# Turning quantized tokens: two DMA transposes per tile in place of eight TensorE transposes

## The chip, the cores and the metric

The kernel runs on one core of a Trainium2 chip. The metric is the device time of one execution in microseconds (us), the median of three runs. A change of under 0.5% (3.2 us here) can't be told from no change.

## The reference

The input `x` is 64 batches of 64 channels by 1024 positions. Two layers follow each other. Cut to what matters for this change, the first one is:

```python
def _L0_cond_ref(x, c, weight, c_weight, bias):      # grouped convolution, 4 groups, 9 taps, pad 4
    out = lax.conv_general_dilated(x, weight, (1,), [(4, 4)], dimension_numbers=('NCH', 'OIH', 'NCH'), feature_group_count=4)
    return out + jnp.einsum('nd,od->no', c, c_weight)[:, :, None] + bias[None, :, None]

def _L0_ffn_ref(input_act, weight):                  # 8 bit quantized dense layer over the 1024 positions
    w_scale = max(abs(weight), axis=-1) / 127;  w_q = round(weight / w_scale)
    a_scale = max(abs(input_act), axis=-1) / 127;  x_q = round(input_act / a_scale)
    return (x_q @ w_q.T * a_scale * w_scale.T).astype(float16)

x = x + _L0_ffn_ref(_L0_cond_ref(x, ...), L0_ffn_weight)
x = x + _L1_ffn_ref(_L1_cond_ref(x, ...), ...)       # per batch 64x64 channel mixing, then a dense layer with a low-rank term
```

A token is one batch and channel (4096 in all), a row of 1024 positions. The dense layer contracts over positions. Its left operand on TensorE must therefore have positions on the partitions and tokens along the free dimension. The convolution leaves the opposite: partitions hold 8 position phases by 16 channels, and the free dimension holds, for each of 8 sets (2 batches by 4 groups), 128 positions of one phase. So each tile has to be turned between the convolution and the integer product, and this step is what changes.

## The kernel before

The work is cut into 32 tiles of two batches (128 tokens). All five engines run hand-written instruction lists. The main loop has one pass for each `c` from 3 to 31. In pass `c`, TensorE (PE) does in this order: the convolution of tile c (`conv`, L462), the channel mixing of tile c-3 (`mix`, L505), the integer product of tile c-2 (`int_product`, L521, 16 matmuls of 512 columns) with the small `row_total` (L485) after the first four and `max_rows` (L528) after eleven, then `max_back` (L532), then `tokens_out` of tile c-1 (L493, the eight transposes) and, in odd passes from 5 on, `rank_pair` (L552, L555). After the loop comes a second stage in which TensorE does the last tiles and then the dense products of layer two (L584, L770); it lasts from 312 us to the end.

Beside it, within a pass:

- VectorE (DVE) adds the bias to the convolution's result (L1245), takes row maxima (L1251), computes the scale of tile c-3 (L1281 to L1288), scales the first half of the product (`layer0(c-2, 0)`, L1277), and then does `chan_max(c)` (L1256, L1257), `low` (L1293), `scales(c)` (L1262, L1263, L1268), and `layer0(c-2, 1)` (L1277 again). DVE works strictly in this order.
- ScalarE (ACT) does `row_sums` (L841), one or two weight steps, `high` twice (L856), `tokens_sb(c-1)` (L846), and `scale_rows(c)` (L863, eight instructions that write `yv`).
- GpSimd (POOL) adds layer one's result to `x` (L1088).
- SyncE (SP) issues DMAs: per pass `save_x1` (L307), which waits for POOL, `save_x2` (L311), the next `x_phases` (L259) and `x` (L263), and in part of the passes a weight tile (L319, L326). One queue keeps them in the order of issue.

The path of a tile's tokens: `scale_rows(t)` in pass t rounds the numbers by adding a large constant, and leaves them in `yv` as f32 words whose lower half is a float16. In pass t+1, TensorE transposes eight 128x128 blocks of these halves into a PSUM bank, and ACT copies the bank into `yq_both` in bf16, taking away the constant. In pass t+2 `int_product` loads `yq_both` as stationary operand. `max_back` brings the channel maxima back to the partitions: DVE makes an 8x128 tile from 8 rows, TensorE turns it into a 128x8 one.

Two waits matter below. `max_back` waits for `chan_max` (semaphore `chanmax_ready`). And `conv(t)` waits, ahead of its third group (g = 2), for `f_ready` 2t-4, that is for `layer0(t-3, 1)`: the second half of the product lies in the PSUM bank that these groups write. In passes with a `rank_pair` that product lies between `max_back` and the next convolution, in the others nothing but `tokens_out` does.

## Time and profile before

| | |
|---|---|
| median of 3 runs | 648.31 us (647.93 to 650.51) |
| profiled execution, span | 646.6 us |
| rest (median less span) | 1.7 us |
| PE busy | 623.8 us, 96% |
| DVE, ACT, POOL busy | 418.3, 335.3, 336.2 us |
| main loop, passes 3 to 31 | some 45 to 312 us |
| DMA | 138.38 MB, mean 214 GB/s |

The profiled execution's own time is given only as its span, from the first to the last instruction; what lies around it is taken as the difference to the median. "PE" is the matmul row and "PEld" the loads of stationary operands, which run ahead of the matmuls. A busy PE is not one at its peak, so gaps in the PEld rows, and the distance from one group's first load to the next one's, say more of what an instruction costs than busy time does. A start is in us from the span's start. "[0.42 <-X]" is an idle time ahead of an instruction, and what ended it.

### The profile page before, as it was taken

The page shows a single profiled execution, that of the slowest core. Times are in us where ns is not written, and L with a number is a line of the kernel's source. Part 1 is how long each engine was busy: PE and PEld are TensorE (multiplying, and loading weights), DVE is VectorE, ACT ScalarE, POOL GpSimd, SP SyncE. Part 2 cuts the span into 40 slices and gives each one's busy share as a digit, 9 for nine tenths or more (in the row PEclk, how much of TensorE's full clock was granted, in tenths as well). Part 3 has the DMA queues.
Part 4 walks back from the last instruction along what each step waited for, and adds up shares of the span by engine and source line. Part 5 has one row for each costly group of instructions (what it writes and reads, how often), then busy time and mean ns, then how long its engine had stood idle before and what let it go on. Part 6 is the DMA issues. An engine that isn't in the chain of part 4 may idle for free.

```text
span 646.6 us, 14948 instructions
## 1 busy us (share of the span) xinstructions
PE 623.8 (96%) x5865; PEld 337.3 (52%) x5898; DVE 418.3 (65%) x891; ACT 335.3 (52%) x566; POOL 336.2 (52%) x223
## 2 busy tenths in 40 slices
PE   7789999999999999999999999999999999999997
PEld 5556565566566666656554444444444444444443
DVE  5958778877787778787537797745544433444434
ACT  2857898667778777776652436334333313333100
POOL 3012222217778522225485689886866678666400
PEclk8799999999999999999999999999999999999999
DMA  8969877677799797764529014554555433457103
GB/s 299 361 137 365 295 284 273 233 266 276 280 342 336 285 359 280 259 229 140 217 73 357 35 34 153 206 203 156 196 195 193 158 132 136 162 197 259 66 1 130
DMA packets 46707, 138.38 MB, mean 214 GB/s; under 512 B 13180, under 2 KB 13468, under 8 KB 46465
## 3 DMA queue, kind: packets, MB, share of 16 engines
q1 hardware_dynamic: 41886, 120.65, 52.6%
q10 hardware_dynamic: 4752, 16.78, 6.4%
q8 instruction: 47, 0.77, 0.5%
q14 instruction: 22, 0.18, 0.1%
HBM read 89.13 MB, written 48.28 MB: 213 GB/s over the span
## 4 chain that ended last, share of the span: by engine, by line
PE 51%; DVE 1%; issue 0%; ACT 0%; DVEq 0%
PE ps L770 36%; PE ps L584 9%; PE ps L752 2%; PE ps L521 2%; PE ps L505 1%; PE ps L462 0%; PE ps L552 0%; DVE z_lo L1304 0%; DVE unscale L1441 0%; DVE ring L1293 0%; DVE yb L1245 0%; DVE zT L1306 0%; PE ps L555 0%; PE ps L730 0%; PE ps L493 0%
## 5 line engine op out<-in xcount | busy, mean ns | idle before, releaser
L1088 POOL TENSOR_TENSOR x<-x_in,f_both 128x512 f32<-128x512 f32 x64 | 74.0, 1157 | 195.9 <-DVE f_both L1277 195.9
L521 PE MATMUL ps<-wqT,yq_both 128*128 128x512 bf16 x479 | 113.2, 379 | 6.0 <-issue 4.6
L462 PE MATMUL ps<-x_ph,conv_w 64*64 64x256 f32 (+1 forms) x1024 | 98.2, 396 | 2.2 <-DMA conv_w<-in_conv_taps 2.0
L863 ACT ACTIVATE yv<-yb,yinv 128x128 f32<-128x128 f32 x256 | 78.0, 389 | 2.3 <-DVE yinv L1268 2.2
L902 ACT ACTIVATE ring<-ring,ratio 128x2048 f16<-128x2048 f16 x26 | 50.6, 1994 | 51.1 <-DVE wst L1537 14.1
L770 PE MATMUL ps<-ffn_wT,ring 128*128 128x512 f16 x312 | 71.6, 379 | 0.0
L462 PEld LDWEIGHTS ps<-x_ph,conv_w 64*64 64x64 f32 (+1 forms) x1024 | 51.1, 137 | 37.4 <-issue 14.2
L521 PEld LDWEIGHTS ps<-wqT,yq_both 128*128 128x128 bf16 x512 | 45.2, 97 | 48.4 <-issue 1.0
L1245 DVE TENSOR_TENSOR yb<-ps,ybias 128x1024 f32<-128x1024 f32 x32 | 39.1, 1223 | 41.1 <-PE ps L462 41.0
L584 PE MATMUL ps<-ffn_wT,ring 128*128 128x512 f16 x288 | 64.6, 379 | 0.0
L856 ACT ACTIVATE ring<-ps,t_up 128x512 f16<-128x512 f32 x64 | 40.5, 683 | 45.5 <-issue 38.1
L1119 POOL TENSOR_TENSOR bias_b<-ring 128x1024 f32<-128x1024 f16 x13 | 27.8, 2137 | 48.4 <-ACT ring L902 48.2
L1550 DVE SCALAR_TENSOR_TENSOR x_in<-ps,unscale,x_in 128x512 f32<-128x512 f32 x30 | 22.5, 750 | 43.7 <-PE ps L770 43.5
L1277 DVE SCALAR_TENSOR_TENSOR f_both<-ps,tok_scale,wsc_b 128x512 f16<-128x512 f32 x64 | 47.8, 748 | 4.1 <-PE ps L521 3.3
L770 PEld LDWEIGHTS ps<-ffn_wT,ring 128*128 128x128 f16 x312 | 30.5, 98 | 36.8
L846 ACT ACTIVATE yq_both<-ps 128x1024 bf16<-128x1024 f16 x32 | 32.7, 1023 | 31.3 <-PE ps L493 31.0
L1293 DVE SCALAR_TENSOR_TENSOR ring<-ps,t_up,ring 128x512 f16<-128x512 f32 x64 | 46.9, 737 | 0.8 <-ACT ring L856 0.8
L584 PEld LDWEIGHTS ps<-ffn_wT,ring 128*128 128x128 f16 x288 | 27.2, 98 | 32.1 <-issue 0.8
L1550 DVE SCALAR_TENSOR_TENSOR wst<-ps,unscale,wst 128x512 f32<-128x512 f32 x28 | 21.0, 750 | 35.2 <-PE ps L770 35.1
L1251 DVE TENSOR_REDUCE rowmax<-yb 128x8 f32<-128x1024 f32 x32 | 39.0, 1220 | 1.0
L505 PEld LDWEIGHTS ps<-mixT,x 64*64 64x64 f32 x2048 | 35.8, 135 | 5.2 <-issue 1.6
L1550 DVE SCALAR_TENSOR_TENSOR x<-ps,unscale,x 128x512 f32<-128x512 f32 x21 | 15.8, 750 | 31.1 <-PE ps L770 31.1
(284 smaller groups left out, 1096.6 us busy)
## 6 DMA issues: line engine op xcount, KB each, us to landing
x_ph<-in_x_phases SPq DMA_DIRECT2D x32, 516.0 KB, 6.1
x_in<-in_x SPq DMA_DIRECT2D x32, 512.0 KB, 6.4
x_scratch<-x SPq DMA_DIRECT2D x32, 512.0 KB, 2.8
x_scratch<-ring SPq DMA_DIRECT2D x26, 512.0 KB, 4.1
ring<-x_scratch SPq DMA_DIRECT2D x26, 512.0 KB, 4.3
wst<-in_w_rows SPq DMA_DIRECT2D x12, 512.0 KB, 5.0
x_in<-x_scratch SPq DMA_DIRECT2D x12, 512.0 KB, 6.5
out<-x_in ACTq DMA_DIRECT2D x12, 512.0 KB, 3.6
```

What stands on the lines that cost most here:

```text
L462: return mm(ps_conv[o, g * 2 * MB:(g + 1) * 2 * MB], conv_w[k, g, w.start + o.start:w.start + o.stop], xp[k, g, :, view], start=first, sto ...
L505: last = mm(bank(2 + e)[j * 64:(j + 1) * 64, k * CH:(k + 1) * CH], x1[b, t % 2, l:l + 64], mixT[b, t, b], start=True, stop=True)
L521: last = mm(acc_bank(t, h), yqT[:, t % 2, p, :], wqT[:, p, h * HALF:(h + 1) * HALF], start=p == 0, stop=p == PH - 1)
L584: last = mm(o, x2_cols[:, x2_slot(n), a, k, :], ffn_wT[:, w, k, h * HALF:(h + 1) * HALF], start=k == 0 and i == 0, stop=k == NL - 1 and i ...
L770: last = mm(b, left(a, k), right(w, k), start=fresh and k == 0 and i == 0, stop=k == 3 and i == 2, skip_group_check=True)
L856: A(x2_cols[:, t % RING, 0, :, h * CH:(h + 1) * CH], bank(2 + h).rearrange("p (c t) -> p c t", c=NL), ACT.Copy, scale=t_up[:, t % 4:t % 4 ...
L863: last = A(yv[:, s, :], yb[:, t % 2, s, :], ACT.Copy, scale=yinv[:, s:s + 1], bias=MAGIC)
L902: A(cols, cols, ACT.Copy, scale=ratio[:, t:t + 1]).then_inc(sem("norm_ready"), 1)
L1088: g.tensor_tensor(x1[:, t % 2, s], x_in[:, t % 3, s], f16[:, s], ALU.add).then_inc(sem("x1_ready"), 1)
L1277: v.scalar_tensor_tensor(f16[:, s], acc_bank(t, h), tok_scale[:, t % 4:t % 4 + 1], wsc_b[:, s], ALU.mult, ALU.mult).then_inc(sem("f_ready" ...
L1293: v.scalar_tensor_tensor(x2_cols[:, t % RING, 1, :, cols], bank(2 + h).rearrange("p (k t) -> p k t", k=NL), t_up[:, t % 4:t % 4 + 1], x2_c ...
L1550: v.scalar_tensor_tensor(buf, src, unscale[:, t:t + 1], buf, ALU.mult, ALU.add).then_inc(sem("pair_folded"), 1)
```

## The change

For tiles 2 to 31 the transposes leave TensorE. ACT writes `yv` less the constant as bf16 into a new tile `yq_out` (`tokens_whole`), at the place where it copied the PSUM bank before. SP then issues two DMA transposes of 64x1024 each into `yq_both` (`turn_tokens`), and `int_product` waits for both. Tiles 0 and 1 (`EARLY = 2`) are turned on TensorE as before.

A DMA transpose of 64 rows gives tokens in another order than the eight TensorE transposes did, so the rows of the convolution's output are reordered: the partition is now (half, channel, phase in the half) where it was (phase, channel). The taps, the bias weights and `fside` are laid out for it ahead of the kernel, and the product's left operand is read with a step of four elements. The scale of a token was found with a masked sum over `ps_small` and `set_mask`; in the new order it comes from a second small product (`chanmax_tok` by `ones8`) in `max_back`, for which `chan_max` has one more instruction.

```diff
+            def turn_tokens(t):
+                sp.wait_ge(sem("yq_ready"), t + 1 - EARLY)
+                wait(sp, "acc_ready", 2 * (t - 1))
+                for h in range(2):
+                    sp.dma_start_transpose(yq_both[:, t % 2, h * HALF:(h + 1) * HALF].rearrange("m (s r) -> m s r", s=8),
+                                           yq_out[h * CH:(h + 1) * CH, :]).then_inc(sem(f"yqT_moved{t % 2}"), 16)
+
             for c in range(1, NT + 3):
+                if c == NT:
+                    turn_tokens(NT - 1)
...
+                if EARLY < c < NT:
+                    turn_tokens(c - 1)
                 if c == NT:
                     fetch_x1(0)
                     load_t(1)
...
             def int_product(t, h, lo=0, hi=PH):
                 if lo == 0:
-                    wait(pe, "yqT_ready", t + 1)
+                    if t < EARLY:
+                        pe.wait_ge(sem("yqT_ready"), t + 1)
+                    else:
+                        pe.wait_ge(sem(f"yqT_moved{t % 2}"), 32 * ((t - EARLY) // 2 + 1))
...
-                    last = mm(acc_bank(t, h), yqT[:, t % 2, p, :], wqT[:, p, h * HALF:(h + 1) * HALF], start=p == 0, stop=p == PH - 1)
+                    last = mm(acc_bank(t, h), yqT[:, t % 2, p // 4, :, p % 4], wqT[:, p, h * HALF:(h + 1) * HALF], start=p == 0, stop=p == PH - 1)
...
             def max_back(t):
-                wait(pe, "chanmax_ready", t + 1)
-                tr(ps_small[:, 128:136], chanmax_rep[:, :, :].rearrange("p a c -> p (a c)"), ident[0:8, 0:8]).then_inc(sem("max_psum"), 1)
+                wait(pe, "chanmax_ready", 2 * t + 2)
+                tr(ps_small[:, 128:136], chanmax_rep[:, :, :, :].rearrange("p h c q -> p (h c q)"), ident[0:8, 0:8])
+                mm(ps_small[:, 136:137], chanmax_tok[:, :, :].rearrange("p s c -> p (s c)"), ones8[:, :], start=True, stop=True).then_inc(sem("max_psum"), 1)
...
                 max_back(c)
-                tokens_out(c - 1)
...
+            def tokens_whole(t):
+                wait(act, "yv_ready", t + 1)
+                if t > EARLY:
+                    act.wait_ge(sem(f"yqT_moved{(t - 1) % 2}"), 32 * ((t - 1 - EARLY) // 2 + 1))
+                A(yq_out[:, :], yv[:, :, :].rearrange("p s m -> p (s m)"), ACT.Copy, bias=-WHOLE).then_inc(sem("yq_ready"), 1)
...
-                tokens_sb(c - 1)
+                tokens_whole(c - 1)
                 scale_rows(c)
 
+            tokens_whole(NT - 1)
             t_high(0)
...
             def chan_max(t):
...
+                v.tensor_tensor(chanmax_tok[:, :, :], chanmax[:, :].unsqueeze(1).to_broadcast([8, 8, CG]),
+                                ident[0:8, 0:8].unsqueeze(2).to_broadcast([8, 8, CG]), ALU.mult).then_inc(sem("chanmax_ready"), 1)
...
-                v.tensor_tensor_reduce(tok_junk[:, :], ps_small[:, 128:136], set_mask[:, :], scale=1.0 / QMAX, scalar=0.0,
-                                       op0=ALU.mult, op1=ALU.add, accum_out=tok_scale[:, t % 4:t % 4 + 1]).then_inc(sem("tok_scale_ready"), 1)
+                v.tensor_scalar(tok_scale[:, t % 4:t % 4 + 1], ps_small[:, 136:137], 1.0 / QMAX, None, ALU.mult).then_inc(sem("tok_scale_ready"), 1)
```

TensorE before, from one pass with a `rank_pair` to the next convolution (L532 is `max_back`, L493 the eight transposes, L552 and L555 the rank pair, L462 the convolution, L505 the mixing, L521 the integer product):

```order
L521 MATMUL ps<-wqT,yq_both 128x512 x5
L532 MATMUL ps<-ident,chanmax_rep 128x8
L493 MATMUL ps<-identh,yv 128x128 x8
L552 MATMUL ps<-ring,z_w 104x256 x8
L555 MATMUL ps<-ring,z_w 40x256 x8
L462 MATMUL ps<-x_ph,conv_w 64x256 x16
L505 MATMUL ps<-mixT,x 64x64 x32
```

The same place after (lines of the changed program: L549 and L550 are `max_back`, L568 and L571 the rank pair, L476 the convolution, L519 the mixing):

```order
L538 MATMUL ps<-wqT,yq_both 128x512 x5
L549 MATMUL ps<-ident,chanmax_rep 128x8
L550 MATMUL ps<-ones,chanmax_tok 128x1
L568 MATMUL ps<-ring,z_w 104x256 x8
L571 MATMUL ps<-ring,z_w 40x256 x8
L476 MATMUL ps<-x_ph,conv_w 64x256 x16
L519 MATMUL ps<-mixT,x 64x64 x32
```

The eight transposes are gone and one small product stands behind `max_back`'s transpose.

VectorE before, around `chan_max` and `scales`:

```order
L1277 SCALAR_TENSOR_TENSOR f_both<-ps,tok_scale,wsc_b 128x512
L1256 TENSOR_REDUCE chanmax<-ps 8x16
L1257 TENSOR_TENSOR chanmax_rep<-ps,chanmax 8x128
L1293 SCALAR_TENSOR_TENSOR ring<-ps,t_up,ring 128x8x64
L1262 TENSOR_SCALAR yscale<-ps 128x8
L1263 ISA tok_junk,tok_scale<-ps,set_mask 128x8
L1263 ISA tok_scale 128x1
L1268 RECIPROCAL yinv<-yscale 128x8
L1277 SCALAR_TENSOR_TENSOR f_both<-ps,tok_scale,wsc_b 128x512
```

And after (L1300 is `layer0`, L1316 `low`):

```order
L1300 SCALAR_TENSOR_TENSOR f_both<-ps,tok_scale,wsc_b 128x512
L1278 TENSOR_REDUCE chanmax<-ps 8x16
L1279 TENSOR_TENSOR chanmax_rep<-ps,chanmax 8x128
L1281 TENSOR_TENSOR chanmax_tok<-chanmax,ident 8x128
L1316 SCALAR_TENSOR_TENSOR ring<-ps,t_up,ring 128x8x64
L1286 TENSOR_SCALAR yscale<-ps 128x8
L1287 TENSOR_SCALAR tok_scale<-ps 128x1
L1291 RECIPROCAL yinv<-yscale 128x8
L1300 SCALAR_TENSOR_TENSOR f_both<-ps,tok_scale,wsc_b 128x512
```

One instruction more stands ahead of `low`, and the masked sum with its readout has become one `TENSOR_SCALAR`.

SyncE before, one pass (the saves of x1 and x2, two loads, a weight tile):

```order
L307 DMA x_scratch<-x 128x1024
L311 DMA x_scratch<-ring 128x1024
L259 DMA x_ph<-in_x_phases 128x1032
L263 DMA x_in<-in_x 128x1024
L319 DMA wst<-in_w_rows 128x1024
```

And after:

```order
L310 DMA x_scratch<-x 128x1024
L314 DMA x_scratch<-ring 128x1024
L262 DMA x_ph<-in_x_phases 128x1032
L266 DMA x_in<-in_x 128x1024
L322 DMA wst<-in_w_rows 128x1024
L373 DMA_TRANSPOSE yq_both<-yq_out 128x8x64 x2
```

The two transposes stand behind the pass's loads and ahead of the next pass's saves.

## Rows read from the trace of the kernel before

**Rows 1.** The page, part 1: engine, busy us, share of the span, instructions.
```profile
PE 623.8 (96%) x5865; PEld 337.3 (52%) x5898; DVE 418.3 (65%) x891; ACT 335.3 (52%) x566; POOL 336.2 (52%) x223
```

**Rows 2.** Waits from 50 to 320 us: who <- for whom: total us, times, longest.
```profile
ACT yq_both L846 <- PE ps L493: 25.8, 24, 1.4
PEld ps L532 <- DVE chanmax_rep L1257: 12.5, 29, 0.6
...
PEld ps L462 <- DVE f_both L1277: 3.9, 14, 0.6
```

**Rows 3.** Timeline, a pass with a rank pair: start us, us, engine, line, operation.
```profile
199.38 1.24 ACT L856 ACTIVATE ring<-ps,t_up 128x512 f16<-128x512 f32 x2
...
200.76 0.13 PEld L532 LDWEIGHTS ps<-ident,chanmax_rep 8*128 8x128 f32 x1 [0.42 <-DVE chanmax_rep L1257]
...
200.91 0.45 PEld L493 LDWEIGHTS ps<-identh,yv 128*128 128x128 f16 x8
...
201.32 0.84 PEld L552 LDWEIGHTS ps<-ring,z_w 128*104 128x104 f16 x8
...
203.51 0.33 SPq L307 DMA_DIRECT2D x_scratch<-x  x1
...
206.57 0.55 PEld L521 LDWEIGHTS ps<-wqT,yq_both 128*128 128x128 bf16 x4
```

**Rows 4.** Timeline, the next pass, without a rank pair.
```profile
208.91 1.27 ACT L856 ACTIVATE ring<-ps,t_up 128x512 f16<-128x512 f32 x2 [0.86 <-issue]
...
209.70 0.28 DVE L1257 TENSOR_TENSOR chanmax_rep<-ps,chanmax 8x128 f32<-8x128 f32 x1
209.91 0.73 DVE L1293 SCALAR_TENSOR_TENSOR ring<-ps,t_up,ring 128x512 f16<-128x512 f32 x1
210.27 0.13 PEld L532 LDWEIGHTS ps<-ident,chanmax_rep 8*128 8x128 f32 x1 [0.42 <-DVE chanmax_rep L1257]
...
210.42 0.45 PEld L493 LDWEIGHTS ps<-identh,yv 128*128 128x128 f16 x8
...
210.57 0.14 DVE L1262 TENSOR_SCALAR yscale<-ps 128x8 f32<-128x8 f32 x1
...
210.98 0.63 PEld L462 LDWEIGHTS ps<-x_ph,conv_w 128*64 128x64 f32 x8
...
211.01 0.75 DVE L1277 SCALAR_TENSOR_TENSOR f_both<-ps,tok_scale,wsc_b 128x512 f16<-128x512 f32 x1
211.09 1.02 ACT L846 ACTIVATE yq_both<-ps 128x1024 bf16<-128x1024 f16 x1 [0.91 <-PE ps L493]
...
211.81 0.66 PEld L462 LDWEIGHTS ps<-x_ph,conv_w 128*64 128x64 f32 x8 [0.21 <-DVE f_both L1277]
...
215.15 0.55 PEld L521 LDWEIGHTS ps<-wqT,yq_both 128*128 128x128 bf16 x4
```

**Rows 5.** DMA issues by tile: count, KB each, median us to landing.
```profile
mixT<-agg_scratch SPq DMA_DIRECT2D x4, 256.0 KB, 4.3
...
out<-wst ACTq DMA_DIRECT2D x2, 256.0 KB, 2.2
```

**Rows 6.** The line of the mixT loads (L297), all four: duration ns, time to landing.
```profile
L297 SPq DMA_DIRECT2D mixT<-agg_scratch x4: 674/1332/1462, 33.9 to 37.4; - x4
...
DMA to landing us min/median/max: 3.5/4.3/4.7
```

**Rows 7.** Timeline of passes 4 and 8: the token copy and the next integer product.
```profile
63.99 1.02 ACT L846 ACTIVATE yq_both<-ps 128x1024 bf16<-128x1024 f16 x1
...
67.17 0.55 PEld L521 LDWEIGHTS ps<-wqT,yq_both 128*128 128x128 bf16 x4
...
101.14 1.02 ACT L846 ACTIVATE yq_both<-ps 128x1024 bf16<-128x1024 f16 x1
...
103.55 0.55 PEld L521 LDWEIGHTS ps<-wqT,yq_both 128*128 128x128 bf16 x4
...
105.59 0.18 PE L485 MATMUL ps<-x1sum,ones_b 128*128 128x1 bf16 x1 [0.99 <-ACT f_both L841]
```

**Rows 8.** Timeline, the last tile's transposes, after the loop.
```profile
320.02 0.65 PEld L493 LDWEIGHTS ps<-identh,yv 128*128 128x128 f16 x8
```

**Rows 9.** The line of the weight transposes (L431), loads with a step of 32 bytes.
```profile
L431 PEld LDWEIGHTS ps<-identh,ffn_wT x64: 140/151/168, 14.7 to 35.9; 128*128 128x128 f16 x64
```

More of the change, by code:

```diff
@@ L34 @@
 HALF_BIAS = 1536.0
-MAGIC = 12582912.0 + 0x6600
+WHOLE = 12582912.0
+MAGIC = WHOLE + 0x6600
 EXPMASK = 0x7F800000
 TOP = 13
+EARLY = 2
 RING = 6
@@ L91, in program @@
         yq = yv[:, :, :].bitcast(F16).rearrange("p s (m w) -> p s m w", w=2)[:, :, :, 0]
-        yqT = yq_both[:, :, :].rearrange("p a (s m) -> p a s m", s=PH)
+        yqT = yq_both[:, :, :].rearrange("m a (h n q) -> m a h n q", h=2, q=PH // 2)
+        yq_out = sb("yq_out", [P, L], BF16)
         f_both = sb("f_both", [P, 2, L], F16)
@@ L692, in _ @@
             int_product(NT - 2, 0)
-            tokens_out(NT - 1)
             int_product(NT - 2, 1)
@@ L845, in tokens_sb @@
                 wait(act, "acc_ready", 2 * (t - 1))
-                A(yqT[:, t % 2, :, :].rearrange("m p (s c) -> m s p c", s=8),
-                  ps_trh.rearrange("m (s p c) -> m s p c", s=8, p=PH), ACT.Copy, bias=-HALF_BIAS).then_inc(sem("yqT_ready"), 1)
+                A(yq_both[:, t % 2, :].rearrange("m (h s r) -> m s h r", h=2, s=8),
+                  ps_trh.rearrange("m (s h r) -> m s h r", s=8, h=2), ACT.Copy, bias=-HALF_BIAS).then_inc(sem("yqT_ready"), 1)
+            def tokens_whole(t):
[3 more added lines that the diff above has]
+                A(yq_out[:, :], yv[:, :, :].rearrange("p s m -> p (s m)"), ACT.Copy, bias=-WHOLE).then_inc(sem("yq_ready"), 1)
             def high(t, h):
@@ L860, in scale_rows @@
                 wait(act, "yinv_ready", t + 1)
-                wait(act, "yqT_psum", t)
+                wait(act, "yqT_psum", min(t, EARLY))
+                wait(act, "yq_ready", t - EARLY)
                 for s in range(8):
-                    last = A(yv[:, s, :], yb[:, t % 2, s, :], ACT.Copy, scale=yinv[:, s:s + 1], bias=MAGIC)
+                    last = A(yv[:, s, :], yb[:, t % 2, s, :], ACT.Copy, scale=yinv[:, s:s + 1], bias=MAGIC if t < EARLY else WHOLE)
                 last.then_inc(sem("yv_ready"), 1)
@@ L990, in _ @@
             t_scale(1)
-            tokens_sb(NT - 1)
             t_scale(2)
@@ L1059, in _ @@
             g = nc.gpsimd
+            g.memset(ones8[:, :], 1.0)
             g.memset(ident[:, :], 0.0).then_inc(sem("ident_zero"), 1)
@@ L1255, in chan_max @@
                 wait(dve, "max_psum", t)
-                link(v.tensor_reduce(chanmax[:, :], ps_small[0:8, 0:P].rearrange("p (a c) -> p c a", a=PH), AX.X, ALU.max))
-                v.tensor_tensor(chanmax_rep[:, :, :], ps_small[0:8, 0:P].rearrange("p (a c) -> p a c", a=PH),
-                                chanmax[:, :].unsqueeze(1).to_broadcast([8, PH, CG]), ALU.max).then_inc(sem("chanmax_ready"), 1)
+                rows = ps_small[0:8, 0:P].rearrange("p (h c q) -> p h c q", h=2, q=PH // 2)
+                link(v.tensor_reduce(chanmax[:, :], rows.rearrange("p h c q -> p c h q"), AX.XY, ALU.max))
+                v.tensor_tensor(chanmax_rep[:, :, :, :], rows, chanmax[:, :].unsqueeze(1).unsqueeze(3).to_broadcast([8, 2, CG, PH // 2]),
+                                ALU.max).then_inc(sem("chanmax_ready"), 1)
+                v.tensor_tensor(chanmax_tok[:, :, :], chanmax[:, :].unsqueeze(1).to_broadcast([8, 8, CG]),
+                                ident[0:8, 0:8].unsqueeze(2).to_broadcast([8, 8, CG]), ALU.mult).then_inc(sem("chanmax_ready"), 1)
             def scales(t):
@@ L1621 @@
         taps[v, :, 2:4, v:v + TAPS] = wc[:, 2:4]
+    taps = taps.reshape(PH, CG, GRP, 4, PH // 2, CG).transpose(0, 1, 2, 3, 5, 4)
     limes4 = _np.zeros((4, 4, E, 4, R), _np.float32)
@@ L1626 @@
         condT=f["cond_128"].T,
-        w_ctx=_np.broadcast_to(f["L0_cond_c_weight"].T.reshape(P, GRP, 1, CG), (P, GRP, PH, CG)).reshape(P, GRP * P),
-        fside=_np.tile(f["fside_S_0"].reshape(GRP, CG).T, (PH, 1)),
+        w_ctx=_np.broadcast_to(f["L0_cond_c_weight"].T.reshape(P, GRP, 1, CG, 1), (P, GRP, 2, CG, PH // 2)).reshape(P, GRP * P),
+        fside=_np.broadcast_to(f["fside_S_0"].reshape(GRP, CG).T.reshape(1, CG, 1, GRP), (2, CG, PH // 2, GRP)).reshape(P, GRP),
         mw0=f["L1_cond_W0"], mw1=f["L1_cond_W1"], mw2=f["L1_cond_W2"],
```

9 lines of the change are left out of this document (3 added, 6 removed).

## The prediction

> **What bounds the kernel now.** I read the page first: the reader is to see PE at 96% of the span while no other engine passes 65% [rows 1]. So TensorE's own list sets the time, and the question for each edit is what it does to the distance from one group of loads to the next on that engine. Next the waits inside the loop [rows 2]. Two of them hold TensorE: `max_back` waits for `chan_max` in all 29 passes, 12.5 us together, and the convolution waits 14 times (3.9 us) for the second half of `layer0`, which happens in the passes without a rank pair. ACT waits 25.8 us for the transposes, but nothing in these rows says that TensorE waits for what ACT does after them. Last, the timeline of one pass of each kind [rows 3, 4], to see what stands ahead of and behind the transposes.
>
> **What leaves TensorE.** In a pass with a rank pair the eight loads start at 200.91 and the next group at 201.32: 0.41 us [rows 3]. Without one it is 210.42 to 210.98, 0.56 us [rows 4]. The last tile's, in the stage behind the loop, take about 0.65 [rows 8], taken as 0.6. Taken by itself this is 14 x 0.41 + 15 x 0.56 + 0.6 = 14.7 us, and it is the whole of what the change can give.
>
> **What `max_back` gets.** The new small product has a load of the shape of L532's (8x128, f32, 0.13 us), and from that load to the next group passes 0.15 us (200.76 to 200.91) [rows 3]. It costs 0.15 us in each pass. The new DVE instruction has the shape of L1257, and from that one to the next instruction on DVE passes 0.21 us (209.70 to 209.91) [rows 4]. `max_back` waits for it too, and this wait is exposed already (0.42 us idle, rows 3 and 4), so 0.21 us is added to TensorE's idle time in full. The masked sum and its readout become one instruction; the reciprocal still waits for it, and I count nothing.
>
> In a pass with a rank pair the sum is -0.41 + 0.15 + 0.21 = -0.05 us. 14 of them: -0.7 us. Pass 3 has 16 small products behind `max_back` and counts the same.
>
> In a pass without one, TensorE comes to the next convolution 0.20 us earlier, but there it meets the wait that was binding before. `layer0` starts at 211.01, 0.44 us after `yscale` at 210.57, and ends at 211.76; the third group's load starts at 211.81 [rows 4]. `yscale` needs the result of `max_back`: 0.30 us after its load (210.27) before; now that load comes 0.21 later and the second product's 0.15 after it, so 0.36 us later. DVE is itself no longer busy then (`low` ends 0.21 later than 210.64). Taking 0.03 off for what DVE was late by before, `layer0` ends 0.33 us later and so does the load of the third group. TensorE's earlier arrival is spent waiting: the pass gets 0.33 us longer. 14 passes: +4.6 us.
>
> Ahead of the loop tile 2 meets the longer wait once, +0.4. The last tile's transposes leave -0.6. Together: -0.7 - 0.05 + 4.6 + 0.4 - 0.6 = +3.7 us. The gain of 14.7 us is gone before any DMA is counted, since 29 x 0.36 = 10.4 us goes to the small product and its input and the rest to the convolution's wait.
>
> **ACT.** `tokens_whole` takes the place of `tokens_sb` at about the same 1.02 us [rows 4] and no longer waits for TensorE: it starts when `high` ends, 0.9 us earlier (210.2 against 211.09). ACT's time isn't on the path, so this gives nothing in itself, but it starts the new DMA earlier.
>
> **The DMA transposes.** `int_product` now waits for them. Cover: in the pass without a rank pair, `high` ends at 210.18, the bf16 tile is there at 211.25, the product's first load stands at 215.15, 0.33 later after the change: 4.2 us. With one: 200.62, 201.7, 206.57: 4.9 us, about 5.1 where ACT is less loaded. SP is free at that moment, since it waits for POOL until 203.51 [rows 3]; behind the transposes on SP stand the saves, and they are late only if the issue takes over 1.8 us. The cover is less in early passes, where ACT has other work between `high` and the tokens: in pass 4, 67.17 less 65.05 is 2.1 us (2.4 with the later load), in pass 8, 103.55 less 102.2 is 1.3 us (1.7) [rows 7]; passes 5 to 7 lie between these and 4.2.
>
> No row shows a DMA transpose. From below: 256 KB in long rows landed 2.2 us after issue on a quiet queue [rows 5]. From above: a mixT load has the same 256 KB, in runs of 32 floats (128 bytes), which is also what a partition gets of one block here (64 tokens of 2 bytes); it took up to 1.46 us to issue and landed in 3.5 to 4.7 us, with four in flight [rows 6]; the sum of both is 6.2. The nearest row is the mixT load with the fewest ahead of it, so I take 3.5 us for the pair. Below the cover of 4.2 nothing is paid in 24 passes. Early passes pay: pass 4 1.1, pass 6 0.5, pass 8 1.8 less the 0.99 that TensorE waited there a moment later anyway (105.59) [rows 7], together 2.4 us.
>
> The VectorE page of the Trainium skill (VectorE: DVE Perf Modes, The three transpose paths) gives 1309 ns for a 128x128 bf16 block through DMA against 390 on TensorE, and its table says to use TensorE when PSUM will do. No run here shows the DMA figure. The eight blocks of this trace cost TensorE 0.41 to 0.56 us together, not 8 x 390 ns, so the price that the rule sets against the DMA is far too high here. By the page's figure, with the blocks one after another, a tile would take an estimated 10.5 us. The same skill (Advanced Engine Details and Errata, X-Bar Transpose) says that on this chip transposing DMAs are as fast as regular ones, which would make it the 2.2 us row.
>
> **Other edits.** The product reads its stationary operand with a step of 8 bytes. Loads with a step of 32 bytes took 0.15 us where others take 0.10 [rows 9, 4], and they lie beside matmuls of 512 columns; I count nothing. If that cover failed it would be up to 0.05 x 480 = 24 us. Layout changes of the taps cost nothing.
>
> **The sum.** On the profiled execution: 646.6 + 3.7 + 2.4 = 652.7 us of span, and with the 1.7 us between span and median 654.4 us.
>
> **Rivals.**
>
> 1. *The saving counts.* If the second small product and its input disappear in time that is idle anyway (the 0.42 us of `max_back`'s wait, if DVE's order gives it back), and only the 0.15 us load is paid, then 14.7 - 29 x 0.15 = 10.3 us is won less what early tiles pay: 640 us. For it speaks that TensorE is at 96% and that the instructions really leave its list. Against it: the 12.5 us wait on DVE and the 3.9 us wait of the convolution, both behind the point where the work is taken away. It decides if the third group's load comes no later than 1.5 us after `max_back`'s.
>
> 2. *The transposes land late.* At 5.6 us (1.33 issue plus 4.3) passes without a rank pair pay 1.4, those with one 0.5, the early ones 14 us together: 14.5 + 4.8 + 14 + 3.7 = +37, 685 us. At 5.0 us it is +23, 671 us. It gets worse in passes where weight loads were issued just before. From 4.2 us on it decides. If the eight blocks went one by one, at 10.5 us, each pass would be some 6 us longer, about +170 us; this is the case that the VectorE page's figure makes. For it: the short runs of [rows 6] are the nearest thing in the trace. Against it: each of the two DMAs has only half of a mixT load's bytes, and the four mixT loads were issued behind each other.
>
> 3. *Nothing to see.* The added wait is smaller than 0.21, or ACT's earlier finish helps TensorE in the early passes; the parts cancel within 3 us.
>
> **Chances.** Forecast (transposes mostly hidden, the gain eaten by the two waits, 650.5 to 660) 0.45. Rival 1 (637 to 645) 0.16. Rival 2 (above 660) 0.23, with 0.03 of it for the long end. Rival 3 (645 to 651.5) 0.16. 0.5% of 648.3 is 3.2 us, about what this measurement can tell from no change. So faster (below 645.1) 0.16; within it 0.22, rival 3 and the lower edge of the forecast; slower 0.62. For 8 in 10 the range goes from 643 (a part of rival 1 below it) to 674 (the upper part of rival 2 above it).
>
> **What would show it.** Right: `max_back`'s load waits about 0.63 us in place of 0.42; in passes without a rank pair the convolution's third group waits some 0.7 us for `layer0`; the pair of passes takes 0.28 us more; from ACT's bf16 tile to landing about 3.5 us; the first load of the product waits for DMA only in passes 4 to 8. Wrong: a wait of each product for `yq_both`, which is rival 2; passes shorter by 0.3 us or more, which is rival 1; loads of the product's left operand over 0.2 us.

## The result, and the profile after: 6.6% slower

| | before | after |
|---|---|---|
| median of 4 executions | 648.12 us (647.85 to 650.51) | 690.99 us (690.03 to 693.41) |
| profiled execution, span | 646.6 | 688.2 |

The ratio is 1.066, 95% interval 1.063 to 1.069. The direction was forecast. The size, +42.9 us where +6.1 was the sum, lies outside the range of 643 to 674.

The page's part 1 of after, against [rows 1]:

```profile
PE 629.0 (91%) x5689; PEld 341.6 (50%) x5722; DVE 443.4 (64%) x890; ACT 336.9 (49%) x566; POOL 336.4 (49%) x224
```

TensorE has fewer instructions than before and is as busy as before, but over a longer span. So it waits, and the waits from 50 to 320 us say for whom (total us, times, longest). On the load row of after, against [rows 2]:

```profile
PEld ps L549 <- DVE chanmax_tok L1281: 23.7, 25, 1.5
...
PEld ps L538 <- DMA yq_both<-yq_out: 11.9, 8, 2.5
...
PEld ps L476 <- DVE f_both L1300: 10.7, 14, 1.1
```

The same view for the matmul row of after, and then what it has on `max_back` for before:

```profile
PE ps L538 <- DMA yq_both<-yq_out: 12.5, 7, 2.7
PE ps L549 <- DVE chanmax_tok L1281: 11.8, 25, 1.0
PE ps L476 <- DVE f_both L1300: 4.4, 13, 0.7
PE ps L538 <- issue: 4.1, 12, 1.4
```

```profile
PE ps L532 <- DVE chanmax_rep L1257: 0.2, 1, 0.2
```

This last row is what the prediction had not read. The loads of `max_back` stood idle for 12.5 us before [rows 2], but the array behind them did not: its matmul row waited 0.2 us in all. After, both rows wait.

The pass without a rank pair of after, against [rows 4] (L1278, L1279 and L1281 are `chan_max`, L549 and L550 `max_back`, L867 `tokens_whole`):

```profile
212.86 0.28 DVE L1278 TENSOR_REDUCE chanmax<-ps 8x16 f32<-8x128 f32 x1
212.93 1.16 POOL L1110 TENSOR_TENSOR x<-x_in,f_both 128x512 f32<-128x512 f32 x1 [1.13 <-DVE f_both L1300]
213.11 1.06 ACT L867 ACTIVATE yq_out<-yv 128x1024 bf16<-128x1024 f32 x1
213.17 0.28 DVE L1279 TENSOR_TENSOR chanmax_rep<-ps,chanmax 8x128 f32<-8x128 f32 x1
213.38 0.85 DVE L1281 TENSOR_TENSOR chanmax_tok<-chanmax,ident 8x128 f32<-8x128 f32 x1
...
214.19 2.51 SPq L373 DMA_TRANSPOSE yq_both<-yq_out  x2
214.28 0.13 PEld L549 LDWEIGHTS ps<-ident,chanmax_rep 8*128 8x128 f32 x1 [0.86 <-DVE chanmax_tok L1281]
214.28 0.22 PE L549 MATMUL ps<-ident,chanmax_rep 8*128 8x8 f32 x1 [0.39 <-DVE chanmax_tok L1281]
214.29 0.35 PEld L550 LDWEIGHTS ps<-ones,chanmax_tok 8*128 8x128 f32 x2
...
214.66 0.63 PEld L476 LDWEIGHTS ps<-x_ph,conv_w 128*64 128x64 f32 x8
...
215.25 0.75 DVE L1300 SCALAR_TENSOR_TENSOR f_both<-ps,tok_scale,wsc_b 128x512 f16<-128x512 f32 x1
...
216.05 0.63 PEld L476 LDWEIGHTS ps<-x_ph,conv_w 128*64 128x64 f32 x8 [0.76 <-DVE f_both L1300]
...
220.58 0.58 PEld L538 LDWEIGHTS ps<-wqT,yq_both 128*128 128x128 bf16 x4 [1.25 <-DMA yq_both<-yq_out]
```

Three things are to be seen. `chanmax_tok` takes 0.85 us, not the 0.28 us of its neighbour of the same shape, and it ends (214.23) just after GpSimd's add (214.09). The two transposes keep SyncE's queue for 2.51 us. And the next product waits 1.25 us for their data: 220.58 is 6.4 us after the bf16 tile was there (214.17).

The line of the transposes, and that of `chanmax_tok`, over the whole execution (ns min/median/max):

```profile
L373 SPq DMA_TRANSPOSE yq_both<-yq_out x60: 1194/1257/2315, 58.9 to 352.3; - x60
...
DMA to landing us min/median/max: 2.6/3.8/7.1
```

```profile
L1281 DVE TENSOR_TENSOR chanmax_tok<-chanmax,ident x32: 268/854/958, 19.1 to 344.9; 8x128 f32<-8x128 f32 x32
```

And SyncE's queue (the page's part 3: packets, MB, share of 16 engines), before and then after:

```profile
q1 hardware_dynamic: 41886, 120.65, 52.6%
```

```profile
q1 hardware_dynamic: 74526, 128.52, 61.7%
```

52.6% of 646.6 us is 340.1, 61.7% of 688.2 us is 424.6. The 60 transposes added 84.5 us of all 16 DMA engines, 2.8 us a tile for 262 KB, and 544 packets each. At the rate of everything else on this queue (340.1 us for 120.65 MB) the same bytes would be 0.74 us.

Cutting the span at the first load of the product of pass 3 and of pass 31 shows where in the program the time lies. The experiments below are in the same table, each from its own trace:

| us | up to pass 3 | pass 3 to 31 | from there to the end | span |
|---|---|---|---|---|
| before | 50.3 | 256.0 | 340.3 | 646.6 |
| after | 54.3 | 287.3 | 346.6 | 688.2 |
| pe_turn | 53.6 | 277.5 | 341.1 | 672.2 |
| no_dma | 54.0 | 274.2 | 340.3 | 668.5 |
| unwaited | 52.9 | 272.6 | 346.5 | 672.0 |
| early | 51.8 | 273.2 | 340.2 | 665.3 |
| pe_mask | 53.0 | 262.5 | 340.6 | 656.1 |
| no_dma_mask | 53.3 | 257.3 | 339.9 | 650.4 |
| early_mask | 52.2 | 262.6 | 339.8 | 654.6 |

TensorE's granted clock is not the same in all of these. Up to pass 3 its mean is 0.86 in before and 0.78 in after. From there on it is full (2.4 GHz) in before's trace, while after has three stretches of some 3.4 us at about half (1.2 GHz): from 117.3, 264.1 and 369.9 us, where the view shows 0.51 to 0.52. Each comes as TensorE goes back to work from a wait, of 2.67, 2.67 and 4.15 us. Such a stretch can cost 1.7 us at most, so the three are up to 5 of the 42 us between the two spans. The wait of 4.15 us and its stretch lie behind the loop, and unwaited has a stretch there too, so up to 1.7 us of the 6 us that both are longer in that stage can be clock. What the lower clock costs was not tested by itself.

### The profile page after: what moved, and what is told of

Same layout as the page of the kernel before. It is cut to its first block and busy times, and to the rows that moved or that the text cites. A ratio compares the mean times of both kernels' runs of the same rounds, so it can differ in the third digit from the quotient of the medians.

```text
span 688.2 us, 14655 instructions
## 1 busy us (share of the span) xinstructions
PE 629.0 (91%) x5689; PEld 341.6 (50%) x5722; DVE 443.4 (64%) x890; ACT 336.9 (49%) x566; POOL 336.4 (49%) x224
## 3 DMA queue, kind: packets, MB, share of 16 engines
q1 hardware_dynamic: 74526, 128.52, 61.7%
## 5 line engine op out<-in xcount | busy, mean ns | idle before, releaser
L538 PE MATMUL ps<-wqT,yq_both 128*128 128x512 bf16 x479 | 117.6, 390 | 20.7 <-DMA yq_both<-yq_out 12.5
L476 PE MATMUL ps<-x_ph,conv_w 64*64 64x256 f32 (+1 forms) x1024 | 101.8, 398 | 6.0 <-DVE f_both L1300 5.1
L538 PEld LDWEIGHTS ps<-wqT,yq_both 128*128 128x128 bf16 x512 | 53.7, 116 | 60.5 <-DMA yq_both<-yq_out 11.9
L476 PEld LDWEIGHTS ps<-x_ph,conv_w 64*64 64x64 f32 (+1 forms) x1024 | 51.2, 139 | 44.3 <-issue 15.7
L784 PE MATMUL ps<-ffn_wT,ring 128*128 128x512 f16 x312 | 71.6, 379 | 0.0
L600 PE MATMUL ps<-ffn_wT,ring 128*128 128x512 f16 x288 | 66.3, 386 | 0.0
L1300 DVE SCALAR_TENSOR_TENSOR f_both<-ps,tok_scale,wsc_b 128x512 f16<-128x512 f32 x64 | 47.9, 749 | 7.7 <-PE ps L538 6.6
L1316 DVE SCALAR_TENSOR_TENSOR ring<-ps,t_up,ring 128x512 f16<-128x512 f32 x64 | 47.0, 738 | 0.8 <-ACT ring L876 0.8
L519 PEld LDWEIGHTS ps<-mixT,x 64*64 64x64 f32 x2048 | 35.5, 135 | 5.0 <-issue 1.3
L519 PE MATMUL ps<-mixT,x 64*64 64x64 f32 x2048 | 35.6, 218 | 0.0
```

Of the source, the lines that this page charges most:

```text
L476: return mm(ps_conv[o, g * 2 * MB:(g + 1) * 2 * MB], conv_w[k, g, w.start + o.start:w.start + o.stop], xp[k, g, :, view], start=first, sto ...
L519: last = mm(bank(2 + e)[j * 64:(j + 1) * 64, k * CH:(k + 1) * CH], x1[b, t % 2, l:l + 64], mixT[b, t, b], start=True, stop=True)
L538: last = mm(acc_bank(t, h), yqT[:, t % 2, p // 4, :, p % 4], wqT[:, p, h * HALF:(h + 1) * HALF], start=p == 0, stop=p == PH - 1)
L600: last = mm(o, x2_cols[:, x2_slot(n), a, k, :], ffn_wT[:, w, k, h * HALF:(h + 1) * HALF], start=k == 0 and i == 0, stop=k == NL - 1 and i ...
L784: last = mm(b, left(a, k), right(w, k), start=fresh and k == 0 and i == 0, stop=k == 3 and i == 2, skip_group_check=True)
L1300: v.scalar_tensor_tensor(f16[:, s], acc_bank(t, h), tok_scale[:, t % 4:t % 4 + 1], wsc_b[:, s], ALU.mult, ALU.mult).then_inc(sem("f_ready" ...
```

## The experiments

The theory after the result: two separate costs, an instruction on DVE that GpSimd holds up, and DMA transposes that land after they are wanted. The main rival: the transposes load the DMA engines, and everything on them is late. Line numbers are those of each kernel's own trace.

**pe_turn.** All 32 tiles are turned on TensorE as before, and the rest of the change stays (row order, second product, `chanmax_tok`, stepped loads).

```diff
-EARLY = 2
+EARLY = 32
...
                 max_back(c)
+                tokens_out(c - 1)
...
-                tokens_whole(c - 1)
+                tokens_sb(c - 1)
```

> All 32 tiles are turned by eight transposes on TensorE again (EARLY = 32, tokens_out and tokens_sb back in their old places), but the new row order, the third instruction in chan_max and the second product in max_back stay. Theory 1 (the way of the channel maxima pays a good part: the trace of the changed kernel shows chanmax_rep to max_back 1.11 us where it was 0.57, and the second product 0.23): 29 passes x 0.75 = +22 us and 1 to 2 ahead of the loop, so about 671 us. Theory 2 (only the late transposes cost): near the kernel before, 648 to 652 us.

Measured: 673.76 us (1.0382, 1.0367 to 1.0398). More than half of the loss, 25.4 us, has nothing to do with a DMA transpose.

**no_dma.** The transposes are neither issued nor waited for; TensorE turns only tiles 0 and 1. The tokens of tiles 2 to 31 are left out of the computation.

```diff
-                if EARLY < c < NT:
-                    turn_tokens(c - 1)
...
-                        pe.wait_ge(sem(f"yqT_moved{t % 2}"), 32 * ((t - EARLY) // 2 + 1))
+                    pe.wait_ge(sem("yqT_ready"), min(t + 1, EARLY))
```

> The changed kernel without its DMA transposes: they are not issued, nobody waits for them, and the products of tiles 2 to 31 read the tokens of tiles 0 and 1, so the tokens of these tiles are left out. ACT still writes yq_out. Theory 1: passes pay the longer way of the maxima and save the eight transposes: 14 x 0.77 + 15 x 0.33 = +16 us and 1 to 4 ahead of the loop: 664 to 668 us. Theory 2 (only the DMA costs): 638 to 648 us, the full saving less the second product.

Measured: 669.26 us (1.0316, 1.0294 to 1.0338). Taking away eight transposes a tile on TensorE gave 4.5 us (from pe_turn), and the time lies 1 us above the range of theory 1.

**unwaited.** The transposes are issued, but their data go to a half of `yq_both` that nobody reads; only the last tile's are waited for. Tokens of tiles 2 to 31 are left out.

```diff
-                    sp.dma_start_transpose(yq_both[:, t % 2, ...
+                    sp.dma_start_transpose(yq_both[:, 1, ...
...
-                    if t < EARLY:
-                        pe.wait_ge(sem("yqT_ready"), t + 1)
-                    else:
+                    pe.wait_ge(sem("yqT_ready"), min(t + 1, EARLY))
+                    if t == NT - 1:
                         pe.wait_ge(sem(f"yqT_moved{t % 2}"), 32 * ((t - EARLY) // 2 + 1))
...
-                    last = mm(acc_bank(t, h), yqT[:, t % 2, ...
+                    last = mm(acc_bank(t, h), yqT[:, t if t < EARLY else 0, ...
```

> The DMA transposes are issued as in the changed kernel, but all into one half of yq_both that no product of tiles 2 to 31 reads (they read tile 0's tokens, so these tiles' tokens are left out); only the last product waits for its transposes. If it is the wait for landing that costs: as no_dma plus at most 6 us for weight loads that stand behind the transposes on SP at the end of the loop, 666 to 673 us. If the load on the DMA engines or on SP's queue itself slows the passes by making x and the weights late: 675 us or more.

Measured: 676.33 us (1.0422, 1.0394 to 1.045), 7.1 above no_dma and 14.7 below after. By the number alone this is the second theory's (675 us or more); the table shows where the time lies. In this trace issuing costs nothing inside the loop (272.6 against 274.2). It costs 6.2 us behind it, up to 1.7 of them perhaps by the clock, where the last two tiles' transposes stand on SyncE's queue ahead of weight loads:

```profile
329.75 7.69 SPq L373 DMA_TRANSPOSE yq_both<-yq_out  x4
337.49 0.58 SPq L310 DMA_DIRECT2D x_scratch<-x  x1
338.17 0.38 SPq L358 DMA_DIRECT2D x_ph<-x_scratch  x1
338.65 0.84 SPq L341 DMA_DIRECT2D row_bias<-in_w_rows  x1
```

Counted from the first load of pass 31's product, `row_bias` is issued 13.1 us later here (338.65 less 325.52) and 8.1 us later in no_dma (336.30 less 328.24). In after the chain from it can be followed to TensorE, in the stage behind the loop:

```profile
345.85 7.71 SPq L373 DMA_TRANSPOSE yq_both<-yq_out  x4
...
362.57 1.15 ACT L905 ACTIVATE row_bias<-row_bias,w_up 128x1024 f32<-128x1024 f32 x1 [6.14 <-DMA conv_w<-in_w_rows]
...
369.82 0.18 PE L499 MATMUL ps<-x1sum,ones_b 128*128 128x1 bf16 x1 [4.15 <-ACT f_both L855]
```

The traces account for only a part of the 7.1 us: their spans differ by 3.5 us (672.0 less 668.5), since the profiled execution of unwaited was its fastest (673.77 of 673.77 to 678.09). Where the other executions lose more isn't known; their granted clock is lower too (0.977 to 0.984 against 0.987).

**psum_mask.** The change as it is, with the 8x8 identity that the mask is multiplied with held in PSUM, so `chanmax_tok` has one operand in SBUF.

```diff
+                if t == 0:
+                    tr(ps_small[0:8, 144:152], ident[0:8, 0:8], ident[0:8, 0:8])
...
-                                ident[0:8, 0:8].unsqueeze(2).to_broadcast([8, 8, CG]), ALU.mult).then_inc(sem("chanmax_ready"), 1)
+                                ps_small[0:8, 144:152].unsqueeze(2).to_broadcast([8, 8, CG]), ALU.mult).then_inc(sem("chanmax_ready"), 1)
```

> The changed kernel, but the second operand of chanmax_tok is an 8x8 identity kept in PSUM in place of the one in SBUF. Claim on the mechanism: this DVE instruction takes 0.85 us because it has two SBUF operands and GpSimd's add of x runs at the same time (it took 0.27 us for tiles 0 and 1, where GpSimd stands still); with one operand in PSUM it should take 0.28 us in every pass. If it is only slow by its shape or broadcast, it stays at 0.85. On the time: if the landing of the transposes sets the passes (waits in parallel), little is won, 683 to 689 us; if the two costs add up, 29 x 0.57 = 16.5 us are won, 674 us.

Measured: 682.96 us (1.0522, 1.0501 to 1.0542), 8.0 us won. The line:

```profile
L1283 DVE TENSOR_TENSOR chanmax_tok<-chanmax,ps x32: 264/266/267, 16.9 to 337.2; 8x128 f32<-8x128 f32 x32
```

No execution of it is longer than 267 ns now. The whole spread of 268 to 958 ns came from the second operand's memory. Only 8 us show, because the shorter passes then wait longer for the transposes: 18.2 us on the matmul row from 50 to 320 us, where after has 12.5.

**early.** ScalarE writes a tile's bf16 tokens right behind its `scale_rows`, in the same pass, and SyncE issues the transposes ahead of the pass's `load_x`, so they have some 5 us more before their product. In the same edit the last tile's pair goes the other way on SyncE's queue: it stood ahead of the weight loads behind the loop, and now stands behind them.

```diff
-                tokens_whole(c - 1)
                 scale_rows(c)
+                tokens_whole(c)
...
+                if EARLY < c < NT:
+                    turn_tokens(c - 1)
                 if 3 <= c < NT:
                     load_x(c)
...
             for c in range(1, NT + 3):
-                if c == NT:
-                    turn_tokens(NT - 1)
...
                 if c == NT:
                     fetch_x1(0)
                     load_t(1)
+                    turn_tokens(NT - 1)
```

> The changed kernel, but tokens_whole(c) stands right behind scale_rows(c) on ACT in place of a pass later, and SP issues the two transposes of tile c-1 behind the x_phases load of pass c (the last tile's behind the weight loads of the stage after the loop). The transposes get some 5 us more to land; everything else stays. If their landing against the product's start is what costs (theory 2): the waits of the product go and the time comes to that of unwaited (676.3) less up to 5 us for weight loads that no longer stand behind the transposes, 670 to 677 us. If the transposes' load on the DMA engines limits the passes: 684 us or more, with other waits on DMA in place of these.

Measured: 667.67 us (1.0316, 1.028 to 1.0352), 23.3 below after and level with no_dma. Its trace has no wait of TensorE for `yq_both`, and the stage behind the loop is back at 340.2 us. The same 60 transposes run here, so what the DMAs cost in after was lateness, of tokens and of weights, and not their load on the DMA engines as such. The time is 2 us below the expected range. That holds for passes as long as these, with the held instruction in them; what the DMAs cost in shorter ones, early_mask shows.

**early_mask.** Both edits together, early's and this one:

```diff
-                                ident[0:8, 0:8].unsqueeze(2).to_broadcast([8, 8, CG]), ALU.mult).then_inc(sem("chanmax_ready"), 1)
+                                ps_small[0:8, 144:152].unsqueeze(2).to_broadcast([8, 8, CG]), ALU.mult).then_inc(sem("chanmax_ready"), 1)
```

> early with the identity for chanmax_tok in PSUM. In psum_mask this gave 8 us, since the landing of the transposes was late in parallel. If that is so, it now gives its full price, 29 to 31 x (0.85 - 0.27) = 17 to 19 us: 653 to 658 us. If it gives 8 us again, the two weren't parallel.

Measured: 655.45 us (1.011, 1.0083 to 1.0137). The time is in the range, but not for the reason given: the edit won 12.2 us where 17 to 19 had been put, and early was below its range already. So the two costs did lie in parallel (8.0 us in psum_mask), and a part of the price is still hidden or spent elsewhere.

**late_tok.** On top of it the token's scale leaves `max_back`: `chanmax_tok`, its product and its readout come later in the pass.

```diff
-                wait(pe, "chanmax_ready", 2 * t + 2)
+                wait(pe, "chanmax_ready", t + 1)
...
                 scales(c)
                 layer0(c - 2, 1)
+                if c > 3:
+                    tok_scaled(c - 1)
+                tok_make(c)
```

> early_mask, and the token scale is taken off the way of the channel maxima: max_back waits for chanmax_rep only, chanmax_tok is made on DVE behind layer0(c-2, 1), its product runs on TensorE behind the mixing of the next pass. Theory 1 with its prices (0.21 us more wait in each pass, 0.23 us for the product in the way of layer0 in 14 passes): about 15 x 0.21 + 14 x 0.44 = 9 us less than early_mask, 644 to 649 us, near the kernel before. If the rest of the loss sits elsewhere (row order, stepped loads, DMA load) it stays over 652 us.

Measured: 655.82 us (1.0119, 1.0095 to 1.0144). A miss: nothing was won. Two of its waits in the loop, 50 to 310 us:

```profile
PEld ps L554 <- DVE chanmax_rep L1296: 11.9, 28, 0.6
...
ACT f_both L912 <- DMA row_bias<-in_w_nat: 9.1, 7, 1.6
```

The first row looks like [rows 2] again, and costs the array as little. That made me test how to read it.

**before_swap.** The kernel before, with both waits of [rows 2] taken away: `tokens_out` ahead of `max_back`, `layer0` ahead of `scales`.

```diff
-                max_back(c)
                 tokens_out(c - 1)
+                max_back(c)
...
-                scales(c)
                 layer0(c - 2, 1)
+                scales(c)
```

> The kernel before, without any part of the change, with two pairs of lines swapped: tokens_out(c-1) stands ahead of max_back(c) on TensorE, and layer0(c-2, 1) ahead of scales(c) on DVE. If the idle time at the two waits is what is to be had (0.42 us a pass at max_back, which the transposes now cover, and the convolution's wait on layer0 in 14 passes): 15 x 0.42 + 14 x 0.46 = 12.7 us, 634 to 640 us. If DVE's order or ACT sets the passes: 645 to 650 us.

Measured: 646.50 us (0.9983, 0.9968 to 0.9998), 1.6 us won where 8 to 14 would have come if the idle time were to be had. Its rows for a pass without a rank pair (start, us):

```profile
208.05 1.24 PE L521 MATMUL ps<-wqT,yq_both 128*128 128x512 bf16 x5
208.91 0.65 PEld L493 LDWEIGHTS ps<-identh,yv 128*128 128x128 f16 x8
209.13 0.61 PE L493 MATMUL ps<-identh,yv 128*128 128x128 f16 x8
209.66 0.13 PEld L532 LDWEIGHTS ps<-ident,chanmax_rep 8*128 8x128 f32 x1
```

The transposes' loads now begin at once, but the array is still at the last 512-column matmuls until 209.1 to 209.3, and the eight take 0.75 us on the load row where they took 0.56 [rows 4]. The idle time ahead of `max_back` was the same matmuls running out. Next to nothing was there to win.

**before_l0.** Only the second of these swaps.

```diff
-                scales(c)
                 layer0(c - 2, 1)
+                scales(c)
```

> The kernel before, where DVE does the second half of layer0 of tile c-2 ahead of the scales of tile c; nothing else moves (before_swap also put tokens_out ahead of max_back). The convolution's third group then waits for nothing. If its wait (3.9 us in 14 passes in the PEld row) is idle time of the array: 644 to 646 us. If the loads only waited beside matmuls that still ran, as at max_back in before_swap: 647 to 649 us.

Measured: 647.96 us (0.9987, 0.9974 to 1.0), not to be told from before. Little of the 3.9 us, if any, was idle time of the array.

**pe_mask.** pe_turn with psum_mask's edit, so to the kernel before:

```diff
+                if t == 0:
+                    tr(ps_small[0:8, 144:152], ident[0:8, 0:8], ident[0:8, 0:8])
...
+                v.tensor_tensor(chanmax_tok[:, :, :], chanmax..., ps_small[0:8, 144:152]..., ALU.mult)
```

> All tiles are turned on TensorE (as pe_turn, 673.8 us), and the 8x8 identity that the token mask is multiplied with lies in PSUM, so that the instruction has one operand in SBUF. No DMA takes part. Theory 1: of the 25.4 us that pe_turn is above the kernel before, nearly all is the one DVE instruction that is held beside GpSimd (0.94 us instead of 0.27, in 27 passes; the rest of the wait on the way from max_back to layer0 moves with it): 655 to 658 us. Rival: the second product, the row order and the stepped loads cost more than the instruction: 662 us or above. If all of it was the instruction: 648 to 651.

Measured: 657.77 us (1.0141, 1.0124 to 1.0159), 16.0 below pe_turn. The PE row's wait from 50 to 310 us, pe_turn and then pe_mask:

```profile
PE ps L547 <- DVE chanmax_tok L1283: 13.4, 26, 1.0
```

```profile
PE ps L549 <- DVE chanmax_tok L1285: 0.3, 1, 0.3
```

The load row of pe_mask still shows 11.4 us for the same wait over this stretch. So an added DVE instruction of 0.27 us is hidden there and one of 0.94 us isn't.

**no_dma_mask.** no_dma with psum_mask's edit; again the tokens of tiles 2 to 31 are left out.

> As pe_mask, but tiles 2 to 31 are not turned at all (no transpose on TensorE, none as DMA; their tokens are left out of the computation), so it is the bound for any way that hides the turning in full. With pe_mask it gives what the eight transposes on TensorE are worth once the held instruction is gone. Theory 1: no more than the 4.5 us seen between pe_turn and no_dma, since the convolution's third group waits for layer0: 651 to 653 us. Rival: with the held instruction gone the 14.7 us of transposes count in full: 641 to 645 us.

Measured: 651.39 us (1.0039, 1.0022 to 1.0056). The eight transposes are worth 6.4 us (from pe_mask), and a version that hides the turning in full would still be 3.0 us above the kernel before (1.4 to 3.6 by the interval).

**early_mask_l0.** early_mask with before_l0's edit:

```diff
-                scales(c)
                 layer0(c - 2, 1)
+                scales(c)
```

> As early_mask (DMA transposes issued a half pass earlier, mask in PSUM; 655.5 us) with layer0 of tile c-2 ahead of the scales on DVE. In early_mask the PE row shows 6.1 us of waits of the convolution's third group for layer0 in 13 passes. Theory 1: that is idle time of the array and goes: 648 to 651 us, level with the kernel before. Rival: the scales come 0.75 us later, and ScalarE's yv and what follows it (tokens, transposes, loads on SyncE's queue) with them: 654 us or above.

Measured: 658.59 us (1.0154, 1.0139 to 1.017), slower than early_mask. The wait moved, from the convolution to `row_total` (1.8 us there in early_mask):

```profile
PE ps L498 <- ACT f_both L856: 11.0, 14, 1.5
```

**pe_mask_two.** pe_mask with the second small product issued twice.

```diff
+                mm(ps_small[:, 136:137], chanmax_tok..., ones8[:, :], start=True, stop=True)
                 mm(ps_small[:, 136:137], chanmax_tok..., ones8[:, :], start=True, stop=True).then_inc(sem("max_psum"), 1)
```

> As pe_mask (657.8 us), with the second small product of max_back issued twice in a row. It measures what one such product costs TensorE and the path to layer0. From the trace of after, max_back's load to the next group went from 0.15 to 0.38 us, so 0.23 us in 29 passes and 3 tiles ahead: 664 to 666 us, and then 6 to 7 of the 9.4 us that pe_mask is above the kernel before are this product. Rival: it hides beside the drain of the big product or the wait for layer0: 657 to 660 us, and the 9.4 us lie elsewhere (the instruction on DVE, the step in the product's loads).

Measured: 664.36 us (1.0249, 1.0232 to 1.0267), +6.6 us in 32 tiles, 0.21 us a product. One of them is thus 6.6 of the 9.4 us that pe_mask is above before.

**pe_late.** pe_mask with late_tok's edit, no DMA.

> As pe_mask, with the token's scale taken out of max_back: max_back waits for the rows' maxima alone, chanmax_tok and its product come later in the pass (the edit that turned early_mask into late_tok and won nothing there). No DMA turns tokens here. Theory 1: late_tok won nothing because the DMA queue held its loads; without it the 0.28 us of waiting in 27 passes goes: 649 to 652 us. Rival: a wait of this size ahead of max_back is beside the matmuls that still run, and only the number of small products counts: 655 to 659 us.

Measured: 659.97 us (1.0185, 1.0168 to 1.0202), 2.2 above pe_mask. Theory 1 fell: with no transpose on the DMA queue there is nothing to win at `max_back` either. That it is slower by 2.2 us is unexplained.

## Why the prediction was wrong

The 42.7 us (690.99 less the 648.3 of before in these comparisons) are the sum of four steps, each the difference of two medians measured. A step holds all that its edit changes, the granted clock too (0.975 to 0.982 in after's executions, 0.977 to 0.987 in unwaited's, 0.985 to 0.987 in no_dma's, 0.986 to 0.997 in before's):

| step | from, to | us |
|---|---|---|
| second product, row order, unheld `chanmax_tok`, no turning at all | before, no_dma_mask | +3.0 |
| `chanmax_tok` held up beside GpSimd | no_dma_mask, no_dma | +17.9 |
| transposes issued but not waited for; 6.2 of it by the trace from weights late behind the loop | no_dma, unwaited | +7.1 |
| transposes late for the product | unwaited, after | +14.7 |

**The first step was forecast at +3.7 and is +3.0, partly by luck.** That the gain of 14.7 us would mostly not arrive was right. In passes without a rank pair the convolution's third group waits for `layer0`, and the freed time is spent there: after's load 0.76 us late. What was left by that account was 14 x 0.41 + 0.6 = 6.3 us, and pe_mask less no_dma_mask is 6.4. The second product was forecast at 0.15 us and is 0.21 (pe_mask_two). The 0.21 us for `chanmax_tok`, "added to TensorE's idle time in full", failed as a reading: that idle time was on the load row only. Of pe_mask's 9.4 us the product takes 6.6, so 2.8 us at most are left for the instruction, the row order and the stepped loads together, under 0.1 us a pass. 2.7 of these lie ahead of pass 3 (53.0 against 50.3), where the sum had +0.4; the granted clock there is the same (0.87 and 0.86), and what makes the start slower was not tested.

**The step that failed by the most is the price of `chanmax_tok`.** It was taken from L1257, of the same shape [rows 4]. But L1257 reads `ps` and `chanmax`, and the new one `chanmax` and `ident`, both in SBUF, while GpSimd's add runs. It took 0.27 us in tiles 0 and 1, where GpSimd was idle, and a median of 0.85 over all. psum_mask brings every one to 0.27, and two pairs of kernels price it: 16.0 (pe_turn, pe_mask) and 17.9 us (no_dma, no_dma_mask). The Trainium skill (SBUF — State Buffer, Who interferes with whom) says that a DVE instruction with two SBUF inputs contends with a GpSimd instruction that reads SBUF. The trace agrees: in after 29 of the 32 overlap the add, and each of the 29 ends 0.13 to 0.15 us after it (214.23 after 214.09 in the pass shown). The three that meet no add take 0.27 us; one of them starts at 267.38, when an add has just ended at 267.36. The sum had no term for it, and no rival did.

**The transposes' landing failed on both of its parts.** 3.5 us after issue was taken for the pair. One transpose lands 3.8 us after its issue in the median, up to 7.1, and the second is issued 1.26 us after the first, so a pair takes about 5.1 us by the medians; in the pass shown it is 6.4 from issue to the product's first load, against a cover of 4.2 to 5.1. This was rival 2 ("at 5.0 us it is +23, 671 us"), which had 0.23. Its own price was of the right size: 23 less the 3.7 of the sum is 19 us, and late tokens cost 14.7 us. It would have been more had the held instruction not lengthened the passes; psum_mask won 8 us where pe_mask won 16. The mixT row [rows 6] was the right neighbour, but its upper end, issue and landing added, was the value to take: two DMAs in one queue are issued one after the other, and both must land.

**SyncE's queue was looked at in the wrong place.** "Late only if the issue takes over 1.8 us": it took 2.51 us a pair, and inside the loop unwaited's trace shows no cost of that. Behind the loop it put weight loads 5 us later, and the stage became 6.2 us longer. The sum had -0.6 there.

**What was right.** The stepped loads hardly matter: pe_mask bounds them, with all else, by 2.8 us. ScalarE is off the path in the loop: from 50 to 320 us neither row of TensorE in after has a wait for it.

The 10.5 us a tile estimated from the figure of the Trainium skill (VectorE: DVE Perf Modes, The three transpose paths) did not come true: 6.4 us passed from the bf16 tile to the product's load in the pass shown. Nor did the statement of the Trainium skill (Advanced Engine Details and Errata, X-Bar Transpose) that transposing DMAs are as fast as regular ones: they held the DMA engines 2.8 us a tile, 3.8 times the 0.74 us of other traffic on this queue. That traffic goes in larger packets, 2.9 KB in the mean against 240 bytes.

**What the change could be.** With the transposes early and the mask in PSUM (early_mask, 655.5 us), turning by DMA comes out 2.3 us below turning on TensorE in the same program (pe_mask, 657.8). That isn't clear of the noise: the intervals against before overlap (1.0083 to 1.0137, and 1.0124 to 1.0159). It is 4.1 us above the bound of no_dma_mask. In the pass shown the pair keeps SyncE's queue for 3.26 us, and in the loop (50 to 310 us) ScalarE waits for weight loads that stand behind it; the timeline row and the row of the waits:

```profile
201.18 3.26 SPq L373 DMA_TRANSPOSE yq_both<-yq_out  x2
```

```profile
ACT f_both L896 <- DMA row_bias<-in_w_nat: 7.4, 6, 1.6
```

That this is the 4.1 us wasn't tested. The load of the DMA engines is a rival for it: their busy share in the part from pass 3 to 31, which adds up packet times and so can pass 1, is 0.77 in no_dma_mask and 1.02 in early_mask, and that part is 5.3 us longer. No version of the change beat the kernel before. before_swap, which has no part of the change, is 1.6 us below it, half of what this measurement can tell from no change.

## What to carry to other kernels

Read an idle time ahead of a load on the matmul row as well: here only what waited on both rows was time to be won, and in early_mask_l0 even that moved elsewhere. Price a new DVE instruction by where its operands lie and what GpSimd does beside it, not by its shape; one operand in PSUM was worth 16 to 18 us here without DMA transposes, 12 us with early ones and 8 us in the changed kernel. A DMA that replaces engine work needs its whole path covered, each issue in its queue plus the landing, and it must stand on that queue where nothing urgent is behind it. Both together gave back 23 us with the same traffic: 5 us more time for each pair in the loop, and the last tile's pair moved behind the weight loads. How the 23 us split between the two was not tested.

## What the runs showed of the hardware

- An 8x128 f32 `TENSOR_TENSOR` took 0.264 to 0.267 us with one operand in PSUM, every time. With both in SBUF it took 0.268 us where GpSimd was idle, and up to 0.958 us beside a 1.16 us add there, ending 0.13 to 0.15 us after the add each time (29 of 29 in after).
- A 64x1024 bf16 DMA transpose from SBUF to SBUF took 1.19 us at least to issue, 1.26 in the median, and landed 2.6 us after the issue at best, 3.8 in the median and 7.1 at most. It made 544 packets.
- Loads with a step of 8 bytes took 0.113 us in the median where unstepped ones took 0.098 (the product's loads in after and before). With all else that changed beside them they cost 2.8 us at most.
- The granted clock of TensorE fell to about half for some 3.4 us as it went back to work from waits of 2.67 us (twice) and 4.15 us in after.
